# A Mamba layer and a table-coded feed-forward layer on one core: decode stages in another order, and two convolution blocks of the first tile made by TensorE

## The reference

```python
proj = u @ W_in.T                        # 512 -> z 512, x 512, B 64, C 64, dt 8
xBC = silu(depthwise_conv(xBC, conv_w, 4 taps, causal) + conv_b)
dt = softplus(dt_toks + dt_bias); dA = exp(dt * -exp(A_log))
S = S * dA_t + dt_t * B_t * x_t          # a scan over the tokens, 8 heads
y = (S . C_t + D_param * x) * silu(z);   mamba = y @ W_out.T
gate, up, down: w = lut[idx]             # 16 values, indices 1376 x 512, int32
ffn = (silu(x @ gate.T) * (x @ up.T)) @ down.T
x = x + layernorm(mamba(layernorm(x)));  x = x + layernorm(ffn(layernorm(x)))
```

## Time and profile before

| | us |
|---|---|
| median of 3 runs | 1389.15 (1387.81 to 1389.2) |
| the profiled execution, device time | 1389.16 |
| its span, first to last instruction | 1387.0 |
| TensorE busy in the span | 1302.5 |
| VectorE busy | 973.6 |
| ScalarE busy | 544.9 |
| GpSimd busy | 532.9 |

### The profile page before, as it was taken

How to read it: one execution, slowest core, us unless ns; L and a number is a source line. 1 busy time by engine, 2 the same in 40 slices (tenths; PEclk the granted TensorE clock), 3 DMA queues, 4 the chain that set the end, 5 groups by cost and what they waited for, 6 DMA issues and landing times. The chain is left out here.

```text
span 1387.0 us, 18643 instructions
## 1 busy us (share of the span) xinstructions
PE 1302.5 (94%) x6656; PEld 630.1 (45%) x6656; DVE 973.6 (70%) x1895; ACT 544.9 (39%) x986; POOL 532.9 (38%) x723
## 2 busy tenths in 40 slices
PE   4778898988999999999999999999999999999997
PEld 2334444534444444444444445444444444444443
DVE  7889998998578756875687668865886555544332
ACT  5556576756434234332334243423443223132120
POOL 1433354434434434435333534364345344400102
PEclk9899999989999999999999999999999999999999
DMA  5144234422321224013302330142213212401201
GB/s 170 38 108 104 71 105 107 123 67 78 84 54 31 69 75 87 23 52 107 84 24 61 99 92 23 35 126 61 54 31 88 51 45 45 108 31 31 77 0 53
DMA packets 132812, 96.16 MB, mean 69 GB/s; under 512 B 102000, under 2 KB 102000, under 8 KB 132720
## 3 DMA queue, kind: packets, MB, share of 16 engines
q1 hardware_dynamic: 130832, 94.94, 26.6%
q10 hardware_dynamic: 1888, 0.03, 0.1%
HBM read 54.05 MB, written 16.78 MB: 51 GB/s over the span
## 5 line engine op out<-in xcount | busy, mean ns | idle before, releaser
L1352 PE MATMUL bank<-fxt,ffn_hi 128*128 128x512 f16 (+1 forms) x1408 | 420.3, 380 | 9.1 <-DVE gact L1684 7.5
L1352 PE MATMUL bank<-fxt,ffn_lo 128*128 128x512 f16 (+1 forms) x704 | 267.4, 380 | 0.0
L1352 PEld LDWEIGHTS bank<-fxt,ffn_hi 128*128 128x128 f16 (+1 forms) x1408 | 139.9, 100 | 179.8 <-DVE gact L1684 10.5
L1258 PE MATMUL bank<-mask,diag 128*128 128x416 f16 x640 | 127.7, 354 | 21.1 <-ACT ffn_lo L873 11.4
L646 POOL TENSOR_TENSOR state<-state,ex 64x512 f32<-64x512 f32 x32 | 37.5, 1173 | 262.0 <-PE bank L1315 260.8
L1366 PE MATMUL bank<-ffn_hi,h_hi 128*128 128x512 f16 (+1 forms) x352 | 133.5, 379 | 0.0
L1366 PE MATMUL bank<-ffn_hi,h_lo 128*128 128x512 f16 (+1 forms) x352 | 133.3, 379 | 0.0
L1366 PE MATMUL bank<-ffn_lo,h_hi 128*128 128x512 f16 (+1 forms) x352 | 133.3, 379 | 0.0
L611 POOL TENSOR_TENSOR decay<-causal_h,da 128x1024 f16<-128x1024 f16 x64 | 122.4, 1933 | 22.1 <-PE bank L1319 17.1
L1535 DVE TENSOR_SCALAR mask<-codes_h 128x832 f16<-128x832 f16 x320 | 119.5, 434 | 5.0 <-PE bank L1258 4.6
L1684 DVE SCALAR_TENSOR_TENSOR gact<-gact,bank 128x512 f32<-128x512 f32 (+1 forms) x88 | 60.3, 685 | 86.2 <-ACT gact L912 85.4
(11 more groups left out here) (186 smaller groups left out, 2240.3 us busy)
## 6 DMA issues: line engine op xcount, KB each, us to landing
codes_sb<-codes SPq DMA_DIRECT2D x80, 208.0 KB, 3.5
ures<-u SPq DMA_DIRECT2D x32, 256.0 KB, 3.0
x_scratch<-x SPq DMA_DIRECT2D x32, 256.0 KB, 2.4
ut<-x_scratch SPq DMA_DIRECT2D x16, 512.0 KB, 4.4
xres<-x_scratch SPq DMA_DIRECT2D x32, 256.0 KB, 3.1
out<-dn SPq DMA_DIRECT2D x32, 256.0 KB, 2.0
ut<-u SPq DMA_DIRECT2D x15, 512.0 KB, 4.3
ffn_hi<-w_in_t SPq DMA_DIRECT2D x4, 580.0 KB, 8.6
```

Of the source, the lines that this page charges most:

```text
L1258: last = nc.tensor.matmul(p.bank[:, 0:COLS], diag[:, q].rearrange("p n m -> p (n m)"), mask[:, n, q, j * COLS:(j + 1) * COLS], start=(q == ...
L1352: last = nc.tensor.matmul(bank, wt[:, c0:c0 + w], fxt[:, :, half, k, :], start=(k == 0 and n == 0), stop=(k == KC - 1 and n == 2))
```

## The change

Two things are changed. The code of the stages t = 2 to 7 stays as it was but for one swap on VectorE (`ln_split` of the next tile's first pair now ahead of `y_split`); GpSimd gets a list of its own for the decode stages.

**The first tile's blocks X2 and X3.** ScalarE makes eight 128 x 128 diagonal matrices of tap weights (`tap_diagonals`, in the memory of the first mask buffer). TensorE makes each of the two convolution blocks with four float32 matmuls of 512 columns into PSUM (`conv_by_diagonals`), ScalarE adds the bias (`conv_biased`). VectorE's two `conv` calls for them are gone.

```diff
+                def conv_by_diagonals(f):
+
+                    o = CONV_ORDER.index(f)
+                    p = take(-1, f"c{f}")
+                    n = PE_CONV.index(f)
+                    pe.wait_ge(s_taps, TAPS * (n + 1))
+                    pe.wait_ge(cin_steps.sem, cin_steps.now(0, 2 * o + 2))
+                    for k in range(TAPS):
+                        last = nc.tensor.matmul(p.bank[:], tap_diag[:, n, k, :], conv_in(0, o)[:, k:k + TILE],
+                                                start=(k == 0), stop=(k == TAPS - 1))
+                    last.then_inc(p.filled, 1)
...
+                def tap_diagonals():
+                    act.wait_ge(s_const, 1)
+                    for n, f in enumerate(PE_CONV):
+                        for k in range(TAPS):
+                            nc.scalar.activation(tap_diag[:, n, k, :], ident[:], ACT.Copy,
+                                                 scale=conv_w_sb[:, f, k:k + 1]).then_inc(s_taps, 1)
```

**The lists.** The ring of the banks 3, 6, 7 and TensorE's prologue; z3 is now made in stage 0, behind the first scan:

```diff
-    return [(-1, f"z{c}") for c in range(SUB)] + [(t, f"D{k}{j}") ...
+    return [(-1, name) for name in ("z0", "z1", *(f"c{f}" for f in PE_CONV), "z2", "z3")] + [(t, f"D{k}{j}") ...
...
+                project_conv(0, 2)
                 pe.wait_ge(s_lo, 3)
                 project_z(0, 0)
-                project_conv(0, 2)
+                project_conv(0, 3)
                 project_z(0, 1)
-                project_conv(0, 3)
-                project_z(0, 2)
+                conv_by_diagonals(2)
+                conv_by_diagonals(3)
                 prepare_small(0, 0)
                 segment_sums(0, 0)
-                project_z(0, 3)
                 prepare_x(0, 0)
+                project_z(0, 2)
```

```diff
+                    if count is not None:
+                        for q in range(GROUP):
+                            one_mask(count, q)
+                    dve.wait_ge(y_steps.sem, y_steps.now(t, YSTEPS * c + 1))
                     dve.wait_ge(y_done.sem, y_done.now(t, c + 1))
                     y_steps.inc(nc.vector.tensor_tensor(y[:], y[:], inner_bank[:], ALU.add))
...
+                    if count is not None:
+                        for q in range(GROUP, PAIRS):
+                            one_mask(count, q)
```

```diff
                     if t == 0:
+                        load_pair("u", t + 1, 1)
                         transpose_pair("u", t + 1, 0)
-                        load_pair("u", t + 1, 1)
...
-                    transpose_pair("u", t + 1, 1)
                     if t + 1 < LAG:
                         load_pair("u", t + 2, 0)
+                    transpose_pair("u", t + 1, 1)
```

More of the change, by code:

```diff
@@ L31 @@
 CONV_ORDER = (4, 0, 1, 2, 3)
+PE_CONV = (2, 3)
 MB = -(-INTER // P)
@@ L89, in early_turns @@
 def early_turns():
-    return [(-1, f"z{c}") for c in range(SUB)] + [(t, f"D{k}{j}") for t in range(LAG) for k in range(SUB * STEP) for j in "ab"]
+    return [(-1, name) for name in ("z0", "z1", *(f"c{f}" for f in PE_CONV), "z2", "z3")] + [(t, f"D{k}{j}") for t in range(LAG) for k in range(SUB * STEP) for j in "ab"]
 class Signal:
@@ L676, in add_output, with decode_stage @@
                     res_ready.inc(nc.gpsimd.tensor_tensor(dn[:, c % 2, :], dn[:, c % 2, :], xres[:], ALU.add))
+                def decode_stage(t):
+                    decay_state(t, 0)
+                    segments(t, 1)
+                    if t >= 1:
+                        out_rstd(t - 1, 3)
+                    weights(t, 1)
+                    if t >= 1:
+                        add_residual(t - 1, 3)
+                    pair_rstd("u", t + 1, 1)
+                    decay_state(t, 1)
+                    segments(t, 2)
+                    out_rstd(t, 0)
+                    weights(t, 2)
+                    add_residual(t, 0)
+                    if t >= 1:
+                        pair_rstd("x", t - 1, 0)
+                    decay_state(t, 2)
+                    segments(t, 3)
+                    out_rstd(t, 1)
+                    weights(t, 3)
+                    add_residual(t, 1)
+                    decay_state(t, 3)
+                    segments(t + 1, 0)
+                    out_rstd(t, 2)
+                    weights(t + 1, 0)
+                    add_residual(t, 2)
+                    if t >= 1:
+                        pair_rstd("x", t - 1, 1)
+                    pair_rstd("u", t + 2, 0)
                 def stage(t):
@@ L772, in _ @@
                 pair_rstd("u", 1, 0)
-                segments(0, 0)
                 weights(0, 0)
-                for t in range(TILES):
+                for t in range(LAG):
+                    decode_stage(t)
+                for t in range(LAG, TILES):
                     stage(t)
@@ L931, in decode_stage @@
                     codes_to_half(k + 5)
+                    decoded(t, 2)
                     if t >= 1:
@@ L975, in decode_stage @@
                     decoded(t, 11)
+                    normalise(t, 1)
                     conv_tanh(t + 1, 1)
@@ L999, in decode_stage @@
                     decoded(t, 16)
+                    normalise(t, 2)
                     codes_to_half(k + 20)
@@ L1145, in _ @@
                 nc.scalar.activation(a_sb[:], a_sb[:], ACT.Exp).then_inc(s_alog, 1)
+                tap_diagonals()
                 act.wait_ge(s_convb, 16)
@@ L1374, in stage @@
                     scan(t, 0)
+                    if t == 0:
+                        project_z(0, 3)
                     if dec:
@@ L1631, in y_step, with y_sum @@
                     dve.wait_ge(y_steps.sem, y_steps.now(t, YSTEPS * c + k))
-                def y_sum(t, c):
+                def y_sum(t, c, count=None):
                     half = t % HALVES
@@ L1723, in decode_stage @@
                     k = half_unit_count(t, 0)
-                    y_sum(t, 0)
-                    if t >= 1:
+                    y_sum(t, 0, k + 1)
+                    if t == 0:
+                        z_gate(0, 3)
+                    else:
                         out_stats(t - 1, 3)
-                    if t == 0:
-                        masks(1)
                     y_gated(t, 0)
@@ L1766, in decode_stage @@
                         ln_stats("x", t - 1, 0)
+                    time_steps(t + 1)
                     conv_silu(t + 1, 0)
                     masks(k + 10)
-                    time_steps(t + 1)
-                    masks(k + 11)
                     if t % HALVES == 1:
                         clear_state((t + 1) // HALVES)
-                    y_sum(t, 2)
+                    y_sum(t, 2, k + 11)
                     out_stats(t, 1)
@@ L1791, in decode_stage @@
                         ln_split("x", t - 1, 0, 1)
-                    masks(k + 16)
-                    y_sum(t, 3)
+                    y_sum(t, 3, k + 16)
                     out_stats(t, 2)
@@ L2046, in _ @@
                 conv(0, 1)
+                conv_silu(0, 1)
+                z_gate(0, 0)
                 ln_stats("u", 1, 0)
-                z_gate(0, 0)
-                conv(0, 2)
-                conv_silu(0, 1)
-                conv(0, 3)
+                z_gate(0, 1)
+                out_scale()
                 conv_silu(0, 2)
-                clear_state(0)
-                z_gate(0, 1)
                 conv_silu(0, 3)
```

78 lines of the change are left out of this document (46 added, 32 removed).

## The result

The changed kernel took 1397.57 us in the median of 4 runs (1395.15 to 1401.51), the kernel before 1388.74 beside it (1387.81 to 1389.2): a ratio of 1.0058, interval 1.004 to 1.0077, some 8 us slower. The forecast was 1373.0. The profiled execution took 1395.15, its span 1393.4, so its trace shows 6 of these 8 us.

What follows compares the result with a forecast made beforehand. Up to about 330 us VectorE's list was taken to set the end, later TensorE's matmuls. Terms -5.0 - 0.5 - 2.6 - 1.5 - 4.5 - 1.6 - 0.5 = -16.2 took 1389.16 to 1373.0 us; own range 1367 to 1379, 80% range 1364 to 1386.

Steps and rivals of the forecast that it cites:

- The one swap in the six steady stages I cost at nothing: Steady stages: the swap costs nothing, since VectorE is busy only 665.8 of 1033.0 us there.
- Part 4: Decode scans: four masks moved behind `y_sum`'s first instruction, four behind the state's addition; state ready 1.5 us sooner, -1.5 us.
- Rival A: Decode scans: GpSimd takes a part back, its state decay delaying VectorE 2.5 us at three scans; 1380.5 us, chance 0.22.
- its sign for a wrong part 4: Decode scans: the masks' step is wrong if GpSimd's decays of the state stand at 3 us and more.
- Rival D: Decode scans: VectorE arrives first and waits at the carried product, its filler masks queued behind; 1393 us, chance 0.08.
- Part 1: Prologue: two `conv` calls removed -4.65, silu of C undisturbed -1.6, new waits for ScalarE +1.3; about -5.0 us.
- Rival E: Prologue gives nothing: diagonal products or shared banks make the second block no sooner than VectorE did; 1378 us, chance 0.11.
- Parts 2, 3, 5 and 6: First half of stage 0 -0.5, `time_steps` ahead of silu -2.6, stage 1 -4.5 and -1.6, from 354 us on -0.5.
- Time steps: Decode stages: `time_steps(1)` fills VectorE's 2.6 us wait for ScalarE's tanh in `conv_silu(1, 0)`; -2.6 us.
- ScalarE's list: Stage 1: `decoded(1, 2)` ahead of `normalise_slice` -4.5 us, `normalise(t, 2)` behind `decoded(t, 16)` -1.6 us.
- part 2: First half of stage 0: load's 2.8 us wait goes but ScalarE's longer list gives it back; -0.5 us in all.
- part 6: From 354 us on: next pair's load ahead of a transpose; waits shrink about 1, transpose 0.5 later; -0.5 us.

Runs made afterwards that it cites:

- stages_only: Kernel before with only the changed lists of the decode stages, masks ahead of `y_sum`, old prologue and old steady stages: 0.9938 of before.
- masks_back: Changed kernel without the swap of the steady stages and with the eight masks ahead of `y_sum`, as before: 0.9962 of the kernel before.
- swap_back: Changed kernel with `y_split` ahead of `ln_split` again in the six steady stages: 0.9994 of the kernel before.
- swap_load: Kernel before with the steady-stage swap, and SyncE's load of the next pair ahead of both transposes there: 0.9944 of before, 1383.12 us.
- prologue_only: Kernel before with only the new prologue; decode stages and steady stages as before: 0.9999 of before.
- loads_alone: Kernel before with only SyncE's three loads ahead of the transposes: 0.995 of before.
- masks_alone: Kernel before with only the masks k + 1, k + 6, k + 11 and k + 16 moved into `y_sum`: 1.006 of before.
- one_tap: `masks0_early` with each diagonal convolution made of one matmul in place of four, three taps left out: 0.9962 of the kernel before, 1386.44 us.
- masks0_early: Changed kernel without swap, masks ahead of `y_sum`, GpSimd's old order, plus the first half unit's codes and masks earlier: 0.9942 of the kernel before, 1384.18 us.

## Why the prediction was wrong

The ledger that the runs give, from one kernel to the next by ratios: the lists -8.6 (`stages_only`); the new prologue with them +3.3 (`masks_back`); masks in `y_sum` +4.4 (`swap_back`); the swap +8.9 (the changed kernel). Sum +8.0, the measured ratio is +8.1; the steps are differences of the same ratios, so that they add up is no proof. Each is uncertain by some 2 us. What the prediction had as a gain of 16.2 us came out as a gain of 8.6 for the lists, and as costs for all else.

1. **The step that failed most: "The one swap in the six steady stages I cost at nothing ... that slack hides it."** VectorE's slack hid the instructions, and not what they hold back. I counted the queues for every other move and not for this one: the split of y releases a DMA, and the load that VectorE waits for stands behind it. It cost 8.9 us, and `swap_load` shows the cause: with the load first on the queue the same swap is in a kernel 7.8 us faster than before.
2. **Part 4, "the state is ready by four masks sooner ... -1.5".** The waits for the state went, from 10.9 to 1.8 us. But the price of a mask was taken from a mean (0.37 us), at a place where GpSimd works beside it: four took up to 4.86 us, and TensorE's waits for masks went from 9.6 to 28.6. The step is +4.4 in the changed kernel and +8 to +10 alone. Rival A had the mechanism, with 0.22, in the wrong row: it took the decay of the state, where the segments are what collides. For the same reason its sign for a wrong part 4, decays of 3 us and more, stayed out: they took 1.0 to 1.7 in the decode stages. Rival D's wait came as described; alone it cost nothing, and D, with 0.08, was the only case that had the kernel slower.
3. **Part 1, the prologue, -5.0.** The segments did not "meet another convolution" at the same 3.15: with the diagonals behind them they held it for 4.7, and ahead of a bank that TensorE needs. The gain at the first scan was 0.7, and in `prologue_only` nothing is left of it at the end; with the new lists the prologue even stands at +3.3. The prices of the new work were good: the eight matmuls took 3.60 and 5.11 us, 8.7 for 8.4, and the silu of C 0.69. Where GpSimd's conflict was taken away, VectorE and TensorE waited for as much elsewhere. What it is in the end that holds the second scan stays open. Rival E was right in its number, and in part in its reason: the last block's silu stood at 57.64 us for 58.98, after 3.15 us of waiting for ScalarE, behind a product that had waited 3.06 for a bank.
4. **Parts 2, 3, 5 and 6 together, -0.5 - 2.6 - 4.5 - 1.6 - 0.5 = -9.7; measured -8.6.** The sum is good and the parts only in places. Time steps -2.6: 2.6 by the scans. ScalarE's list -6.1: -5.1. The loads had 2.8 in part 2, which I gave back to ScalarE's list, and 0.5 in part 6; alone they are worth 6.9. At the start of stage 2 I had 0.5 for a wait of 3.04 that fell to 0.9 in `loads_alone`, and there the low clock behind it went too (0.76 and 0.82 in the two stretches of 380 to 388 us, 1.00 in `loads_alone`). That the parts give less together than alone hid this in the sum, so its closeness is in part luck.
5. **The range.** It was built of bounds on the terms that I had. The swap, set at nothing, had none. Part 4 had -4.5 to +1.5, from a mean, and measured +4.4.

## What to carry to other kernels

Price an instruction by the rows of the place that it moves to, not by its mean: who else works there decides whether four masks take 1.2 or 4.9 us. A move on an engine with a third of its time idle is free only if nothing waits for what moves back; follow each result through its DMA queue to the next engine. And when a load and a result-driven transpose share a queue, try the load first: three such moves alone gave 6.9 us in the decode stages, and in the steady stages one turned the swap's loss into a gain.

## What the runs showed of the hardware

Contention between VectorE and GpSimd is a large part of this kernel's time. Cutting GpSimd's segments in the decode stages to a sixteenth gave 15 to 17 us of 1389, though GpSimd is on no long wait of TensorE there. From 50 us to the first scan of stage 2 VectorE was busy 249.5 us in place of 266.9 with the same work. Some of the gain can have come another way, since GpSimd was also done sooner: ScalarE's waits for its `obias` fell from 26.2 to 19.6 us.

The slowing is selective. In the rows of `masks_alone` above, beside the segments from 219.09 to 223.11 us, the two additions with an operand in PSUM took 0.67 and 0.69 us as ever, and the four masks 3.19 for 1.2. In the changed kernel four masks took 4.86 us beside segments of 4.01:

```profile
173.07 4.86 DVE L1618 TENSOR_SCALAR mask<-codes_h 128x832 f16<-128x832 f16 x4
```

```profile
173.70 4.01 POOL L621 TENSOR_TENSOR decay<-causal_h,da 128x1024 f16<-128x1024 f16 x2 [0.25 <-POOL state L656]
```

A trace of one execution is no fine ruler for a prologue: with the same instructions up to there, the first convolution step started 1.2 us later in `one_tap` than in `masks0_early`. TensorE's matmuls of 512 columns still took 0.63 us at 28.26 in the one, and 0.38 from 26.53 on in the other.
